# Graph kernel: ten weight slots, first norm in two rounded passes, two destination blocks kept in PSUM

## The reference

```
node = x @ W1;  hw = einsum('nc,kcf->nkf', x, W2)         # K = 16
x0   = einsum('nk,nkf->nf', node, hw)
x1   = layernorm(x + relu(adj @ x0 + node @ b))
msg  = x1 @ W + B
weights = where(adj < 1, exp(-(1/adj - 1)**2 / 0.5), 0)
out  = layernorm(x1 + weights @ msg)
```

## Time and profile before

| | us |
|---|---|
| median of three runs (lowest, highest) | 579.78 (579.68, 581.64) |
| the profiled execution's own time | 579.95 |
| its span | 577.8 |
| PE, ACT, DVE busy in it | 561.4, 507.7, 491.1 |
| mean granted TensorE clock | 0.989 |

### The profile page before, as it was taken

One profiled execution on the slowest core, in us unless ns is written; L12 is line 12 of the kernel. 1 busy time (PEld: TensorE's weight loads), 2 busy tenths in 40 slices (PEclk: granted clock), 3 DMA queues, 4 the chain that ended last, 5 costly groups with the idle time before them and its releaser, 6 DMA issues.

```text
span 577.8 us, 5251 instructions
## 1 busy us (share of the span) xinstructions
PE 561.4 (97%) x1798; PEld 331.6 (57%) x1798; DVE 491.1 (85%) x542; ACT 507.7 (88%) x464; POOL 82.9 (14%) x74
## 2 busy tenths in 40 slices
PE   9999999999899999999999999999999999889976
PEld 8888888456555655565556555655555565444434
DVE  6777768999879989998999899989998999499742
ACT  5788878799649999989998999899989998999975
POOL 2889999000000000000000000000000000000000
PEclk9999999999899999999999999999999999979999
DMA  5980000689788888888788978887888884435002
GB/s 183 416 353 19 21 0 0 253 339 361 302 304 313 321 295 309 297 325 305 287 319 322 334 276 331 326 300 297 309 314 311 304 301 146 150 145 214 18 36 91
DMA packets 23129, 142.24 MB, mean 246 GB/s; under 512 B 2720, under 2 KB 3136, under 8 KB 6720
## 3 DMA queue, kind: packets, MB, share of 16 engines
q1 hardware_dynamic: 22960, 141.66, 65.3%
...
## 4 chain that ended last, share of the span: by engine, by line
PE 78%; ACT 11%; DVE 6%; issue 3%; DMA 2%; SPq 0%; POOL 0%; DVEq 0%; ACTq 0%; POOLq 0%
PE l_ps L444 29%; PE acc_ps L411 12%; PE hw_ps L374 5%; PE hw_ps L380 5%; PE hw_ps L377 5%; PE acc_ps L400 5%; PE acc_ps L402 5%; PE acc_ps L401 5%; ACT wt_pair L565 3%; ACT wt_pair L570 3%; ACT wt_pair L582 3%; DVE wt_pair L721 2%; DMA row_in<-adjT_dram 2%; PE var_ps L428 1%; PE acc_ps L352 1%
## 5 line engine op out<-in xcount | busy, mean ns | idle before, releaser
L444 PE MATMUL l_ps<-wt_pair,msg 128*128 128x512 f32 x504 | 228.1, 597 | 0.0
L444 PEld LDWEIGHTS l_ps<-wt_pair,msg 128*128 128x128 f32 x504 | 96.2, 192 | 111.8 <-issue 110.1
L715 DVE SCALAR_TENSOR_TENSOR wt_pair<-wt_pair 128x2048 f32<-128x2048 f32 x64 | 146.1, 2283 | 0.0
L565 ACT ACTIVATE wt_pair<-wt_pair 128x4096 f32<-128x4096 f32 (+1 forms) x39 | 116.9, 2997 | 8.7 <-DVE wt_pair L715 8.7
L570 ACT ACTIVATE wt_pair<-wt_pair 128x4096 f32<-128x4096 f32 (+1 forms) x39 | 117.3, 3008 | 1.2
L411 PE MATMUL acc_ps<-row_in,x 128*128 128x512 f32 x208 | 93.2, 592 | 0.0
L582 ACT ACTIVATE wt_pair<-wt_pair 128x4096 f32<-128x4096 f32 (+1 forms) x21 | 62.3, 2968 | 31.6 <-DVE wt_pair L721 31.6
L552 ACT ACTIVATE prods<-hw_ps,node 128x128 f32<-128x128 f32 x256 | 73.2, 374 | 17.1 <-PE hw_ps L380 15.6
L708 DVE TENSOR_TENSOR adj_lo<-row_in,adj_hi 128x2048 fp32r<-128x2048 f32 x38 | 87.1, 2292 | 1.3
L721 DVE SCALAR_TENSOR_TENSOR wt_pair<-wt_pair 128x4096 f32<-128x4096 f32 (+1 forms) x21 | 75.7, 3603 | 3.1 <-ACT wt_pair L570 3.1
L675 DVE SCALAR_TENSOR_TENSOR part_acc<-hw_ps,node,part_acc 128x128 f32<-128x128 f32 x224 | 60.7, 343 | 19.3 <-PE hw_ps L380 19.3
...
## 6 DMA issues: line engine op xcount, KB each, us to landing
...
```

What stands on the lines that cost most here:

```text
L444: mm = pe.matmul(l1_ps[:, t % L1_BANKS, :], msg[:, c % 2, k, :], wt[t % WT_RING][:, k, :], start=(k == 0), stop=(k == CH - 1))
L565: act.activation(w, w, ACT.Ln, bias=TINY).then_inc(ln_made, 1)
L715: dve.scalar_tensor_tensor(out=w, in0=w, scalar=1.0, in1=w, op0=ALU.is_lt, op1=ALU.mult).then_inc(mask_made, 1)
```

## The change

- **Ring of ten.** `WT_RING` goes from 8 to 10, four slots of it late ones, filled at SP's steps 2, 4, 7 and 9. Masks, Ln and inverse of a pair move two steps ahead (`COL_LAG - 6` for `COL_LAG - 4`), and which of two successive pairs VectorE squares is swapped. Only the last four tiles go one by one; tiles 56 to 59 become pairs.
- **First norm in two passes.** y is rounded to float32r (`y_hi`) with its remainder (`y_lo`), and centre is two float32r products with a rounded matrix instead of one float32 product. variance likewise, from `sq_hi` (a second Square on ScalarE) and `sq_lo` (a subtraction on VectorE, `remainder_of_square`).
- **Two blocks kept.** Column tiles of destination blocks 0 and 1 (`KEPT = 2`) accumulate in a PSUM bank each over all eight source blocks and are added to `sumT` once, in the last row. The other six blocks take turns in two banks.
- **Row tiles.** The ring of row tiles has five slots; the remainder of a split tile overwrites the tile in its slot (`row_lo`), so that the slot is free only when TensorE is done with it. In row 1 four tiles are split instead of five, tile 12 is whole.
- `x_row` has one buffer for two, `B_sb` is one chunk, broadcast.

```diff
-ROW_RING = 4
-WT_RING = 8
-LATE_SLOTS = 2
-L1_BANKS = 4
+ROW_RING = 5
+WT_RING = 10
+LATE_SLOTS = 4
+
+KEPT = 2
+L1_BANKS = 2
-SPLIT_FIRST = (3, 5, 7)
+SPLIT_FIRST = ((3, 5, 7), (1, 3, 5, 7))
-LAST_MASKS = (63, 64, 65, 66, 67, 69, 70, 71)
+LAST_MASKS = (65, 66, 67, 68)
...
-LATE_AT = (6, 10)
+LATE_AT = (2, 4, 7, 9)
...
-            return (m - FIRST_PAIR) % 4 < 2
+            return (m - FIRST_PAIR) % 4 >= 2
...
-            step = m + COL_LAG - 4
+            step = m + COL_LAG - 6
...
+    def is_added(t):
+        return t % NB >= KEPT or t >= TILES - NB
...
-                pe.wait_ge(y_made, r + 1)
...
-                pe.matmul(yc_ps[:, :], centre_w[:, :], y[:, :], start=True, stop=True).then_inc(yc_made, 1)
+                pe.wait_ge(y_lo_made, r + 1)
+                pe.matmul(yc_ps[:, :], centre_r[:, :], y_hi[:, :], start=True, stop=False)
+                pe.matmul(yc_ps[:, :], centre_r[:, :], y_lo[:, :], start=False, stop=True).then_inc(yc_made, 1)
...
-                at_least(pe, sum_added, t - L1_BANKS + 1)
+                if j >= KEPT:
+
+                    at_least(pe, sum_added, added_to(t - L1_BANKS - (KEPT if j < KEPT + L1_BANKS else 0)))
+                    out, first, last = l1_ps[:, j % L1_BANKS, :], True, True
+                else:
+                    out, first, last = kept_ps[:, j, :], c == 0, c == NB - 1
...
-                act.activation(sq[:, 0, :], yc_ps[:, :], ACT.Square).then_inc(sq_made, 1)
+                act.activation(sq[0][:, :], yc_ps[:, :], ACT.Square).then_inc(sq_made, 1)
+                act.activation(sq_hi[:, :], yc_ps[:, :], ACT.Square).then_inc(sq_hi_made, 1)
...
+                dve.wait_ge(y_made, r + 1)
+                dve.tensor_copy(y_hi[:, :], y[:, :]).then_inc(y_hi_made, 1)
+                dve.wait_ge(y_hi_made, r + 1)
+                dve.tensor_tensor(y_lo[:, :], y[:, :], y_hi[:, :], ALU.subtract).then_inc(y_lo_made, 1)
+
+            def remainder_of_square(r):
+                dve.wait_ge(sq_made, r + 1)
+                dve.wait_ge(sq_hi_made, r + 1)
+                dve.tensor_tensor(sq_lo[:, :], sq[0][:, :], sq_hi[:, :], ALU.subtract).then_inc(sq_lo_made, 1)
```

More of the change, by code:

```diff
@@ L125, in gnn_kernel @@
         exps_at.setdefault(step, []).append(m)
-    lo_order = [g for g in SPLIT if g in SPLIT_FIRST] + [g for g in SPLIT if g not in SPLIT_FIRST]
+    lo_order = list(dict.fromkeys([i % NB for i in split_tiles]))
     LAST = TILES - 1
@@ L142, in width, with added_to @@
         return BW if u < NB - 1 else HALF_BW
+    def is_added(t):
+        return t % NB >= KEPT or t >= TILES - NB
+    def added_to(t):
+        return len([s for s in range(t + 1) if is_added(s)])
     def row_added_step(r):
@@ L161, in gnn_kernel @@
         sumT = sb("sumT", [P, N])
-        row_in = [sb(f"row_in_{s}", [P, CH, BW]) for s in range(ROW_RING)]
+        with ExitStack() as whole:
+            row_in = [sb(f"row_in_{s}", [P, CH, BW], F32, whole) for s in range(ROW_RING)]
+        row_lo = [sb(f"row_lo_{s}", [P, CH, BW], F32R) for s in range(ROW_RING)]
         wt_pair = [sb(f"wt_pair_{s}", [P, 2, CH, BW]) for s in range((WT_RING - LATE_SLOTS) // 2)]
-        x_row = sb("x_row", [P, 2, BW])
+        x_row = sb("x_row", [P, BW])
         W_sb = sb("W_sb", [P, P])
-        W1_sb = sb("W1_sb", [P, K])
-        W1T_sb = sb("W1T_sb", [K, P])
-        b0_sb = sb("b0_sb", [K, P])
         W1b = sb("W1b", [P, P])
-        B_sb = sb("B_sb", [P, CH, P])
+        B_sb = sb("B_sb", [P, P])
         mean_w = sb("mean_w", [P, P])
@@ L190, in gnn_kernel @@
         y = sb("y", [P, BW])
-        sq = sb("sq", [P, 2, BW])
-        rstd = sb("rstd", [P, 2, BW])
+        with ExitStack() as first_norm:
+            y_hi = sb("y_hi", [P, BW], F32R, first_norm)
+            y_lo = sb("y_lo", [P, BW], F32R, first_norm)
+            sq_hi, sq_lo = y_hi, y_lo
+        odd_sq = sb("odd_sq", [P, BW])
+        odd_rstd = sb("odd_rstd", [P, BW])
+        sq = [sb("sq", [P, BW]), odd_sq]
+        rstd = [sb("rstd", [P, BW]), odd_rstd]
+        mean_r = sb("mean_r", [P, P], F32R)
+        centre_r = sb("centre_r", [P, P], F32R)
         x1T = y
@@ L217, in gnn_kernel @@
         x_in_sem = [sem(f"x_in_{s}") for s in range(2)]
-        x_row_in = [sem(f"x_row_in_{s}") for s in range(2)]
+        x_row_in = sem("x_row_in")
         row_tile_in = [sem(f"row_tile_in_{s}") for s in range(ROW_RING)]
```

115 lines of the change are left out of this document (66 added, 49 removed).

## The result

| | before | after |
|---|---|---|
| median (lowest to highest) of 20 runs each, us | 580.42 (579.26 to 583.01) | 584.08 (580.97 to 585.12) |
| profiled execution: time, span, us | 579.95, 577.8 | 583.79, 581.8 |
| mean granted TensorE clock | 0.989 | 0.983 |

The ratio is 1.005, with a 95% interval of 1.0037 to 1.0063. The forecast was 581.7, in a range of 575.5 to 586.5: the time lies in it, 2.4 above the forecast. It is a small but real loss: the interval leaves out 1, the ratio stands just at the half per cent within which the prediction counted "same", and 584.08 is past the 582.7 from which it counted "slower", so its likeliest range, 577.5 to 582.7, was missed.

The account below looks back on a forecast made before the run. TensorE, busy 97% of the span, was taken to bound the kernel, with ScalarE tying in the middle. Terms 0.1 - 4.4 + 8.4 - 2.2 = +1.9 on 579.95 gave 581.85 profiled, forecast 581.7, range 575.5 to 586.5.

Parts of the forecast that it names:

- Term 1: Start to column tile 8: ScalarE's long waits vanish but it is then busy; TensorE starts the tile at 207.0, +0.1 us.
- Term 2: Middle, to the last centre: five rows at -0.80 us on TensorE and the last centre -0.40, together -4.4 us.
- Term 3: Last centre to `centre2(0)`: 41.3 us for 32.9, behind ScalarE's weights and VectorE's add of tile 56; +8.4 us.
- Term 4: `centre2(0)` to tile 63: weights now early, 3.1 us charged for the slow clock; 29.7 us for 31.9, -2.2 us.
- What it named: Profile signs: no ScalarE wait over 2 us from 105 to 495, 12 to 16 before `centre2(0)`, PEclk 0.50, last exponential near 544.
- cover some 6 us: Two PSUM banks: VectorE's add comes a step and more before the column tile needs it; TensorE waits only for any excess.
- second rival: Column tile 8r waits for `copy_messages`: lateness beyond 0.25 us lost once a row; 1 us a row gives 586.7; chance 0.20.
- low clock: TensorE behind its wait at `centre2(0)`: 3.1 us lost at PEclk 0.50, a longer wait costing no more than a short one.
- first rival: Adds not held back at the end: `centre2(0)` starts at 525, no slow clock, time 566.5; chance 0.10.
- both long waits of ScalarE vanish: Start of the weights: ScalarE's idle 5.39 and 8.76 us go with earlier masks, yet column tile 8 starts at 207.0.

Follow-up runs that it names:

- e1: Changed kernel with the last row's four single tiles moved back between the second norm's steps; 568.90 us, ratio 0.981 to the kernel before.
- e4: Changed kernel with 13 more float32 products on TensorE just ahead of `centre2(0)`, in its wait; 582.29 us, ratio 1.0026 to the kernel before.
- e3: Changed kernel with the first norm's centre and variance in one float32 product each again; 582.72 us, ratio 1.0043 to the kernel before.
- e11: Kernel of e1 with masks, Ln and inverse of pairs two steps later, last four masks at steps 67 to 70; 582.36 us, ratio 1.0038 to before.

## Why the prediction came out as it did

By its own steps, with 1.8 taken off for the start where a time is compared:

| | forecast | measured |
|---|---|---|
| Term 1, start to column tile 8 | +0.1 (207.0) | +0.2 (208.84 - 1.8 = 207.0) |
| Term 2, to the end of the last centre | -4.4 (496.0) | -4.5 (497.8 - 1.8 = 496.0) |
| Term 3, last centre to `centre2(0)` | +8.4 (41.3) | +9.1 (539.74 - 497.80 = 41.9) |
| Term 4, `centre2(0)` to the last tile | -2.2 (29.7) | -2.6 (569.06 - 539.74 = 29.3) |
| sum | +1.9 | +2.2 |
| late start of the profiled execution | none | +1.8 |

- **What it named came about.** No wait of ScalarE over 2 us up to 495 but the one for the very first mask, TensorE's wait of 12.3 us ahead of `centre2(0)` (12 to 16), PEclk 0.50 behind it, the last exponential at 544.7.
- **Term 3** is short by 0.7, and all of it lies ahead of VectorE's square of pair 56: 497.8 in the forecast, 500.20 - 1.8 = 498.4 in the trace. ScalarE was still in an inverse when the centre ended (497.80) and squared from 498.42; the prediction had it ready. From there to `centre2(0)` it is 39.5 in both. The wait of TensorE has its length from the other side: it was done with tile 57 at 527.5 - 1.8 = 525.7 and not at 522.6, mainly because of column tile 53 (next point), so the wait was 12.3 and not 14.7. That moved nothing.
- **Column tile 53** was let off ("cover some 6 us"): the cover was gone once. VectorE's square of pair 56 and a mask stood ahead of the add of tile 51, and TensorE waited 2.2 and ran tile 53 at half clock. It cost nothing, because it lay in front of the 12.3; in e1 no such wait follows it.
- **The greater part of the miss,** 1.8 in the profiled execution, is the start, for which the sum had no term. The trace of before could not show it, being one execution of the early kind; the three times shown, 579.68, 579.78 and 581.64, did.
- **The second rival** (column tile 8r waits for `copy_messages`) came once, 1.7 at tile 8, which is Term 1, and never after.
- **The low clock.** The prediction let the row of a 3.8 us wait stand for a long one. From `centre2(0)` to `centre2(1)` it was 7.0 us after a wait of 12.3 and 6.1 after one of 2.8 (e4), for 4.3 at full clock (e1): 2.7 and 1.8 lost; in e3, after a wait of 13.5, it was 5.8, so 1.5 lost. The Trainium skill (TensorE: Matmul & The Clock Gate, What's actually happening) says that the throttled state is the default and that activity releases it. The traces agree in that a longer wait did not cost more than the 3.1 charged.

**What was wrong in the reasoning, though the sum was right.** First, the terms were read as worth of their own: "Term 2: -4.4" is true of TensorE's time at the last centre, and undoing its cause gave -0.6 (e3; +0.6 without the clock's luck), not +4.4. ScalarE ties with TensorE, and behind the last centre ScalarE's chain sets the end; what the norm saved on TensorE went into the wait. Second, against its first rival the prediction said that ScalarE "would have to be 9 us earlier than its work allows". That holds for the written order alone. In e1 ScalarE does the same work, and from the start of the last centre to that of `centre2(0)` it is 30.5 for 42.8; the squares of the second norm were what had to move. Third, the start: "both long waits of ScalarE vanish. But ScalarE is then simply busy" is right for tile 8, and I took it that the lead was therefore worth nothing. e11 shows it worth 13.3 in all with e1's order: 14.7 at the end and 2.8 in the rows, against 4.2 at the start. In the changed kernel the four tables spend it again.

**Open.** What the ring of five, tile 12 and the single x_row do was not tried alone. The changed kernel's runs fall into the late-start group 13 times in 20 and those of before 9 times in 20 (13 in 29 beside the first experiments); whether that is more than chance is not settled, and it moves the medians.
